# Focal modulation inside a four-block token network: gated maps of two levels added and turned once, rows summed by VectorE, the input turned by 96 products, linear units in 32x32 tiles

## The chip, the cores and the metric

The kernel runs on one core of one Trainium2 chip. The metric is device time in microseconds of one execution. A profile shows five engines: TensorE (PE, its weight loads apart as PEld), VectorE (DVE), ScalarE (ACT), GpSimd (POOL) and SyncE (SP, which here only starts DMAs).

## The reference, cut to what matters

The input is (16, 24, 24, 32): 16 images, 24 x 24 positions, 32 channels. Four blocks follow each other, each with a residual and a norm ahead of it: focal modulation, a recurrence over tokens, a bidirectional state space scan, a mixture of experts. Only the first is changed.

```python
y = einsum('bhwc,cd->bhwd', x, Wf) + bf          # x is the normed input
q, ctx, gates = y[..., :C], y[..., C:2*C], y[..., 2*C:]
ctx_all = 0
for l, k in enumerate((k0, k1, k2)):             # 3x3, 5x5, 7x7, depthwise
    ctx = gelu(dwconv_same(ctx, k))
    ctx_all = ctx_all + ctx * gates[..., l:l+1]
ctx_global = gelu(mean(ctx, axis=(1, 2), keepdims=True))
ctx_all = ctx_all + ctx_global * gates[..., 3:]
x_out = q * (einsum('bhwc,cd->bhwd', ctx_all, Wh) + bh)
x_out = layer_norm(x_out) * gamma + beta         # over channels
x = x + einsum('bhwc,cd->bhwd', x_out, Wp) + bp
```

## The kernel before, in words

Everything stays in on-chip memory. The usual layout, "plain", has partition = group g of images (4) times channel (32), and free = image j in the group (4) times position (576). A position range is worked in two halves a of 288. All products are float32, and each product or weight load of the program leaves two records in the trace.

The first block runs in this order. `ln_pe`, `ln_act` and `ln_dve` are the norm: centring by a product (L391 with full 128x128 tiles, L374 with 32x32 tiles, which also exchanges g and j), a square on ScalarE (L425), a copy (L432), variance (L398), root (L427), reciprocal (L436), spreading (L412) and the final multiplication (L440). `ctx_rows` (L1049) then turns the normed input: for each row y, image j and channel parity c0, a product takes 32 positions as the stationary side and the 76 columns of `wcg` as the moving one, and so writes context channels and gates with the x position on the partitions. `bring_ctx` (L731) adds the bias and moves the result from the banks to `CT0`.

`conv_block` (L1087) does the depthwise convolutions of the three levels with Toeplitz weights in 64x64 tiles, in halves kh of the channels. A record of it has up to 192 moving columns; level 0 has 192 records, level 1 320 and level 2 448. Between blocks, `linear` (L1071) computes q and the part of the global gate in four units of four full products, and `linear_out` (L563) moves each. After each half, ScalarE applies Gelu in two instructions (L571), VectorE multiplies by the gate (`gate`, L750), and after each level VectorE turns the map back with 32x32 transposes in two halves (`turn`, L758). `spread_gates` (L1064) and a ScalarE copy (L556) bring the gates of level 0 and level 2 to the partitions that need them.

After the last convolution TensorE sums the level 2 map over its rows with 48 products against a matrix of ones (L1116). ScalarE takes the Gelu of the mean (L574), VectorE turns and masks it (L766, L770), TensorE makes it a number per channel and image (L1137), and ScalarE moves that (L576). `by_j` (L1122) multiplies the turned maps of the three levels with Wh and adds them up in the banks, one half at a time. VectorE combines this with the global part (L780) and with q (L783) into `XO`, which goes into the next norm. `keep_warm` issues products of zeros (L381) while TensorE would wait.

The order on each engine is the order of the program. SyncE's queue loads, in this order, half of the input, the first weights, the other half, the Toeplitz weights of the three levels, and the weights of later blocks. GpSimd's queue loads `front_in` and `rows_in`. GpSimd computes nothing in the first block but one small fill.

## Time and profile before

| | us |
|---|---|
| median of 3 runs (lowest, highest) | 815.52 (812.94, 819.01) |
| the profiled execution, its time | 813.94 |
| its span, first to last instruction | 812.1 |
| PE busy in the span | 663.8 |
| DVE busy | 619.6 |
| ACT busy | 361.2 |
| POOL busy | 467.7 |
| mean granted TensorE clock | 0.930 of full |

Busy times are sums over the whole kernel, whose blocks have different limits. The first block takes about the first 130 us of the span. A row of a timeline has the start, the time from the first to the last of the merged instructions, the engine, the line, the operation with its operands and shape, the count, and in brackets how long the engine had been idle and what ended that.

### The profile page before, as it was taken

How to read it: one execution, taken by the hardware profiler on the slowest of the kernel's cores; microseconds unless marked ns; L12 is line 12 of the kernel's file. 1: busy time of each engine (PE TensorE's matmuls, PEld its weight loads, DVE VectorE, ACT ScalarE, POOL GpSimd, SP SyncE). 2: the span in 40 equal slices, each digit the busy share in tenths (PEclk: the TensorE clock that was granted, in tenths of full speed). 3: DMA queues.
4: the chain of work that ended last, by engine and by line, in shares of the span. 5: the costliest groups of instructions: out<-in, count | busy, mean ns of one | idle time of the engine just before them, and what ended most of it. 6: DMA issues, size and time to landing. Idle time of an engine off the chain costs nothing. (4 is left out here: it accounts for less than half of the span.)

```text
span 812.1 us, 14545 instructions
## 1 busy us (share of the span) xinstructions
PE 663.8 (82%) x5852; PEld 423.8 (52%) x5852; DVE 619.6 (76%) x664; ACT 361.2 (44%) x569; POOL 467.7 (58%) x239
## 2 busy tenths in 40 slices
PE   7699977899583778988888887898888887786696
PEld 4588933566351455554555555555455454452242
DVE  3254256632431999999999999999999999977765
ACT  2032121566337655645655565565565555422000
POOL 0000000000102899999999999999999999970000
PEclk9799688999798799999999999999999999998577
DMA  9300000000025588797887788778779878710001
GB/s 365 148 3 2 1 2 2 2 0 1 3 74 133 154 209 199 200 227 202 201 227 198 203 226 202 201 205 220 208 200 226 200 204 219 201 47 2 1 17 44
DMA packets 35491, 109.22 MB, mean 134 GB/s; under 512 B 6816, under 2 KB 8992, under 8 KB 35040
## 3 DMA queue, kind: packets, MB, share of 16 engines
q1 hardware_dynamic: 35200, 107.40, 50.4%
q8 instruction: 46, 0.75, 0.4%
q0 software_dynamic: 224, 0.90, 0.3%
q14 instruction: 21, 0.17, 0.1%
HBM read 104.73 MB, written 3.54 MB: 133 GB/s over the span
## 5 line engine op out<-in xcount | busy, mean ns | idle before, releaser
L538 POOL TENSOR_TENSOR ring<-ring,big 128x1152 f32<-128x1152 f32 x74 | 193.9, 2634 | 3.6 <-DVE ring L908 3.6
L197 PE MATMUL banks<-ring,main_params 128*128 128x288 f32 x592 | 173.0, 421 | 0.6 <-POOL ring L538 0.6
L685 ACT ACTIVATE big<-big,small 128x576 f32<-128x576 f32 x192 | 142.5, 765 | 30.4 <-DVE ring L908 15.8
L908 DVE TENSOR_TENSOR_SCAN ring<-big,banks 128x576 f32<-128x576 f32 x111 | 146.1, 1339 | 1.9 <-ACT banks L685 0.4
L896 DVE TENSOR_TENSOR banks<-banks,big 128x576 f32<-128x576 f32 x192 | 141.3, 743 | 1.8 <-POOL big L524 1.6
L1262 PE MATMUL banks<-big,selectors 96*128 96x512 bf16 x192 | 72.5, 389 | 70.5 <-DVE ring L908 40.2
L514 POOL COPY big<-normed 128x288 f32<-128x288 f32 x8 | 3.0, 428 | 214.6 <-DVE normed L440 214.6
L197 PEld LDWEIGHTS banks<-ring,main_params 128*128 128x128 f32 x592 | 104.8, 190 | 35.8 <-issue 3.7
L538 POOL TENSOR_TENSOR normed<-normed,big 128x1152 f32<-128x1152 f32 x36 | 94.6, 2637 | 0.2 <-DVE normed L903 0.2
L197 PE MATMUL banks<-normed,main_params 128*128 128x288 f32 x288 | 83.5, 420 | 0.0
L685 ACT ACTIVATE banks<-big,small 128x576 f32<-128x576 f32 x64 | 47.5, 742 | 79.3 <-DVE ring L908 46.3
L1262 PEld LDWEIGHTS banks<-big,selectors 96*128 96x128 bf16 x192 | 18.5, 96 | 118.5 <-DVE ring L908 59.4
L908 DVE TENSOR_TENSOR_SCAN normed<-big,banks 128x576 f32<-128x576 f32 x54 | 71.2, 1339 | 0.8
L197 PEld LDWEIGHTS banks<-normed,main_params 128*128 128x128 f32 x288 | 51.0, 190 | 16.7 <-issue 1.9
L197 PE MATMUL banks<-big,main_params 128*128 128x288 f32 x208 | 59.6, 416 | 0.0
L381 PE MATMUL banks<-idle 128*128 128x128 bf16 (+1 forms) x172 | 48.0, 341 | 5.6 <-DVE big L968 2.6
L1176 PE MATMUL banks<-big,main_params 128*128 128x90 f32 (+4 forms) x208 | 52.5, 371 | 0.0
L531 POOL TENSOR_TENSOR ring<-big 128x576 f32<-128x576 f32 x37 | 52.1, 1409 | 0.1
L903 DVE TENSOR_TENSOR_SCAN ring<-banks,ring 128x576 f32<-128x576 f32 x37 | 49.6, 1341 | 0.0
L538 POOL TENSOR_TENSOR big<-big 128x1152 f32<-128x1152 f32 x18 | 47.4, 2631 | 0.2 <-DVE big L903 0.2
L518 POOL TENSOR_TENSOR big<-big 128x576 f32<-128x576 f32 x16 | 22.6, 1412 | 38.2 <-ACT big L667 38.2
L197 PEld LDWEIGHTS banks<-big,main_params 128*128 128x128 f32 x208 | 37.3, 190 | 12.0 <-issue 0.9
(186 smaller groups left out, 1043.0 us busy)
## 6 DMA issues: line engine op xcount, KB each, us to landing
big<-bc_rows SPq DMA_DIRECT2D x256, 288.0 KB, 4.4
big<-bc_rows SPq DMA_DIRECT2D x128, 144.0 KB, 4.5
big<-toeplitz_in SPq DMA_DIRECT2D x1, 3584.0 KB, 21.5
bc_rows<-big SPq DMA_DIRECT2D x16, 144.0 KB, 3.5
big<-toeplitz_in SPq DMA_DIRECT2D x1, 1536.0 KB, 10.4
big<-toeplitz_in SPq DMA_DIRECT2D x1, 1280.0 KB, 12.5
residual<-x_in SPq DMA_DIRECT2D x2, 576.0 KB, 5.9
out<-big SPq DMA_DIRECT2D x16, 72.0 KB, 1.8
```

The lines of the kernel that those rows point to most:

```text
L197: last = nc.tensor.matmul(PS[rows, 2 * p + a, 0:HALF], lhsT, rhs[:, bass.ds(at + a * HALF, HALF)], start=start, stop=stop, skip_group_chec ...
L381: nc.tensor.matmul(PS[:, bank, 0:cols], IDLE[:, 0:128], IDLE[:, 0:cols], start=True, stop=True)
L514: nc.gpsimd.tensor_copy(there, XN[:, j * L + a * HALF:j * L + (a + 1) * HALF][:, ::-1]).then_inc(turned, 1)
L518: nc.gpsimd.tensor_tensor(DT[b % 3], DT[b % 3], TMP[b % 2], ALU.add).then_inc(dt_set, 1)
L531: nc.gpsimd.tensor_tensor(SLOT[n % SLOTS], BT[m % 3], DTX[n // DS % 2], ALU.mult).then_inc(u_pool, 1)
L538: nc.gpsimd.tensor_tensor(slots, slots, CT[k % 5], ALU.mult).then_inc(weighted, 1)
L685: nc.scalar.activation(out, DT[b % 3], ACT.Exp, scale=ANEG[:, s:s + 1]).then_inc(decay_set, 1)
L896: nc.vector.tensor_tensor(u, u, DTX[n // DS % 2], ALU.mult).then_inc(u_dve, 1)
L903: nc.vector.tensor_tensor_scan(slot, place, slot, 0.0, ALU.mult, ALU.add).then_inc(scanned, 1)
L908: nc.vector.tensor_tensor_scan(slot, DECAY[m % 3], place, 0.0, ALU.mult, ALU.add).then_inc(scanned, 1)
L1176: nc.tensor.matmul(step_place(k, h), par("vt"), at_step(YP, k, 0, images_of(h)), start=False, stop=True, skip_group_check=True).then_inc(r ...
L1262: nc.tensor.matmul(PS[:, 2 * place, :], lhsT, SPLIT[b % 4][:, 0:BANK], start=True, stop=True)
```

## The change

1. The normed input is written by VectorE into `PADDED`, rows of 32 positions of which 24 are used, two images side by side. GpSimd fills it with zeros first. `ctx_rows` then needs 96 products with 64 stationary columns in place of 192 with 32, and the channel bits stand on other partitions; Toeplitz weights of level 1 double in size, since each half of the partitions has its own.
2. `spread_gates` and its copy go: the gates come out of the turning where they are needed.
3. `linear` uses `strips`, 16 products in 32x32 tiles, which exchange g and j, from `PADDED`; the four units move to other places between the conv blocks. The norm after the modulation so uses full products for the centring, in place of strips.
4. The gated map of level 0 isn't turned: it is added to that of level 2 by VectorE (`add_first`), and the sum is turned. `by_j` has two maps, not three.
5. VectorE sums rows (`sum_rows`, tensor_reduce), and TensorE keeps one product with `sumx`.

```diff
-TW_AT = [0, KS[0] * CP * 64, KS[0] * CP * 64 + KS[1] * KB * 64]
+TW_AT = [0, KS[0] * CP * 64, (KS[0] + KS[1]) * CP * 64]
...
         P0, P1, P2 = CT0[:, 0:TB], A1, B2
-        P0T, P1T = big(TB), big(TB)
+        P1T = big(TB)
+        PADDED = C3
         P2T = P0
         QS = big(N)
         XO = QS
         WPG = big(128)
-        GA = big(2 * 2 * COLS)
-        GG, GGT, GMASK, GADD = big(128), big(128), big(GROUPS * J), big(J)
+        YS, GG, GGT, GMASK, GADD = big(128 + GROUPS), big(128), big(128), big(GROUPS * J), big(J)
...
-        LINEAR = {(1, 0): ("q", 0), (1, 1): ("global", 0), (2, 0): ("q", 1), (2, 1): ("global", 1)}
+        LINEAR = {(0, 1): ("q", 0), (1, 0): ("q", 1), (1, 1): ("global", 0), (2, 0): ("global", 1)}
         LINEARS = list(LINEAR.values())
 
         def by_pair(t):
 
             return t.rearrange("p (n m y) -> p n m y", n=CP, y=H)
+
+        def padded(rows, j, a):
+
+            return PADDED.rearrange("p (b y j x) -> p b j y x", b=2, y=H, j=2)[rows, j // 2, j % 2, a * H // 2:(a + 1) * H // 2, 0:W]
 
...
+                if to_padded:
+                    for b in range(2):
+                        js = slice(2 * b, 2 * b + 2)
+                        here = PADDED.rearrange("p (b y j x) -> p b j y x", b=2, y=H, j=2)[:, b, :, a * H // 2:(a + 1) * H // 2, 0:W]
+                        last = nc.vector.tensor_tensor(here, halves(dst, a)[:, js].rearrange("p j (y x) -> p j y x", x=W),
+                                                       quad(a)[:, js].rearrange("p j (y x) -> p j y x", x=W), ALU.mult)
+                    last.then_inc(ln_out, 1)
+                    continue
...
-            nc.gpsimd.memset(XNW[:, N:N + 8], 0.0).then_inc(tail_zero, 1)
+            nc.gpsimd.memset(PADDED, 0.0).then_inc(pads_zero, 1)
...
-            act.wait_ge(rep_mm, 1)
-            nc.scalar.activation(GA.rearrange("p (l j c) -> p j l c", l=2, j=2),
-                                 PS[:, 4:6, 0:2 * COLS].rearrange("p j (l c) -> p j l c", l=2), ACT.Copy).then_inc(ga_set, 1)
...
-            for kh in range(2):
-                act.wait_ge(sum_mm, kh + 1)
-                nc.scalar.activation(GG[:, 64 * kh:64 * (kh + 1)], PS[:, 4 * kh, 0:64], ACT.Gelu, scale=1.0 / L).then_inc(glob_set, 1)
+            act.wait_ge(sum_mm, 1)
+            nc.scalar.activation(GG, PS[:, 7, 320:448], ACT.Gelu, scale=1.0 / L).then_inc(glob_set, 1)
             act.wait_ge(gadd_mm, 1)
-            nc.scalar.activation(GADD, PS[:, 5, 0:J], ACT.Copy).then_inc(gadd_set, 1)
+            nc.scalar.activation(GADD, PS[:, 7, 448:448 + GROUPS], ACT.Copy).then_inc(gadd_set, 1)
...
-            ln_dve(dve, 0, XN)
+            dve.wait_ge(pads_zero, 1)
+            ln_dve(dve, 0, XN, to_padded=True)
...
-                cols = COLS if l == 1 else 2 * COLS
-                g = CT0[:, (CP + 1) * COLS:(CP + 2) * COLS] if l == 1 else GA[:, l // 2 * cols:(l // 2 + 1) * cols]
+                g = CT0[:, (CP + l) * COLS:(CP + l + 1) * COLS]
+                if l == 1:
+                    dve.wait_ge(gated, 2)
+                dve.wait_ge(ctx_dve, 3)
                 dve.wait_ge(gelu_set, 2 * (2 * l + kh + 1))
-                if l != 1:
-                    dve.wait_ge(ga_set, 1)
-                n = TB // 2 // cols
-                nc.vector.tensor_tensor(dst[:, half].rearrange("p (n c) -> p n c", c=cols),
-                                        src[:, half].rearrange("p (n c) -> p n c", c=cols),
-                                        g.unsqueeze(1).to_broadcast([128, n, cols]), ALU.mult).then_inc(gated, 1)
+                nc.vector.tensor_tensor(dst[:, half].rearrange("p (n c) -> p n c", c=COLS),
+                                        src[:, half].rearrange("p (n c) -> p n c", c=COLS),
+                                        g.unsqueeze(1).to_broadcast([128, CP // 2, COLS]), ALU.mult).then_inc(gated, 1)
...
                 if l == 2:
-                    dve.wait_ge(turned_p, 2)
-                nc.vector.transpose(turned_row((P0T, P1T, P2T)[l], a), by_row((P0, P1, P2)[l], a)).then_inc(turned_p, 1)
+                    dve.wait_ge(added, 2)
+                nc.vector.transpose(turned_row({1: P1T, 2: P2T}[l], a), by_row((P0, P1, P2)[l], a)).then_inc(turned_p, 1)
+
+            nc.vector.memset(YS[:, 128:128 + GROUPS], 0.0).then_inc(summed_c, 1)
+
+            def sum_rows(kh):
+                dve.wait_ge(gelu_set, 2 * (2 * 2 + kh + 1))
+                nc.vector.tensor_reduce(YS[:, 64 * kh:64 * (kh + 1)],
+                                        C3[:, kh * TB // 2:(kh + 1) * TB // 2].rearrange("p (i y) -> p i y", y=H),
+                                        AX.X, ALU.add).then_inc(summed_c, 1)
+
+            def add_first(kh):
+                half = slice(kh * TB // 2, (kh + 1) * TB // 2)
+                dve.wait_ge(gated, 4 + kh + 1)
+                nc.vector.tensor_tensor(P2[:, half], P2[:, half], P0[:, half], ALU.add).then_inc(added, 1)
 
             for l in range(LEVELS):
                 for kh in range(2):
+                    if l == 2:
+                        sum_rows(kh)
                     gate(l, kh)
+                    if l == 2:
+                        add_first(kh)
+                if l == 0:
+                    continue
                 turn(l, 0)
...
-                    dve.wait_ge(glob_set, 2)
+                    dve.wait_ge(glob_set, 1)
...
                 turn(l, 1)
...
-
-            def ctx_rows(ys):
-                for y in ys:
-                    for j in range(J):
+
+            def ctx_rows(a):
+                for y in range(a * H // 2, (a + 1) * H // 2):
+                    for j1 in range(2):
                         for c0 in range(2):
-                            strip = 2 * (j // 2) + c0
-                            here = PS[C * strip:C * (strip + 1), y // 3, 0:3 * CG * 2 * GROUPS]
-                            here = here.rearrange("p (y c q) -> p y c q", y=3, c=CG)[:, y % 3, :, GROUPS * (j % 2):GROUPS * (j % 2 + 1)]
-                            last = nc.tensor.matmul(here, XNW[:, j * L + y * W:j * L + y * W + 32],
-                                                    fpar("wcg")[:, c0 * CG * GROUPS:(c0 + 1) * CG * GROUPS], start=True, stop=True)
+                            w = fpar("wcg")[:, c0 * CG * GROUPS:(c0 + 1) * CG * GROUPS]
+                            here = PS[64 * c0:64 * (c0 + 1), y // 3, 0:3 * CG * 2 * GROUPS]
+                            here = here.rearrange("p (y c q) -> p y c q", y=3, c=CG)[:, y % 3, :, GROUPS * j1:GROUPS * (j1 + 1)]
+                            at = 64 * (j1 * H + y)
+                            last = nc.tensor.matmul(here, PADDED[:, at:at + 64], w, start=True, stop=True)
                 return last
 
-            pe.wait_ge(ln_out, 1)
-            ctx_rows(range(H // 2 - 1))
-            pe.wait_ge(ln_out, 2)
-            ctx_rows([H // 2 - 1]).then_inc(ctx_mm, 1)
-            ctx_rows(range(H // 2, H)).then_inc(ctx_mm, 1)
-
-            def spread_gates():
-                gates = CT0[:, TB:TB + LEVELS * COLS].rearrange("p (l c) -> p l c", l=LEVELS)[:, 0:LEVELS:2, :]
-                pe.wait_ge(ctx_dve, 3)
-                for r in range(2):
-                    rows = slice(64 * r, 64 * r + 32)
-                    last = nc.tensor.matmul(PS[:, 4 + r, 0:2 * COLS], fpar("rep")[rows, :], gates[rows], start=True, stop=True)
-                last.then_inc(rep_mm, 1)
+            for a in range(2):
+                pe.wait_ge(ln_out, a + 1)
+                ctx_rows(a).then_inc(ctx_mm, 1)
 
             def linear(u, q):
                 kind, a = u
                 w = {"q": fpar("wq"), "global": fpar("wg3")}[kind]
-                for j in range(J):
-                    last = nc.tensor.matmul(PS[:, 4 * q + j, 0:HALF], w, XN[:, j * L + a * HALF:j * L + (a + 1) * HALF],
-                                            start=True, stop=True)
+                last = strips(quad_bank(q), own(w), lambda rows, j: padded(rows, j, a), True, True)
                 last.then_inc(lin_mm, 1)
...
-                            n = (dy + KS[l] // 2) * KB + k if l == 1 else (dy + KS[l] // 2) * CP + 2 * k + q
-                            at = TW_AT[l] + 64 * n
+                            at = TW_AT[l] + 64 * ((dy + KS[l] // 2) * CP + 2 * k + q)
...
-                    if (l, kh) == (0, 1):
-                        pe.wait_ge(ga_set, 1)
-                    if l >= 1 and (l, kh) != (1, 0):
-                        pe.wait_ge(lin_act, 2 * l + kh - 2)
+                    if l >= 1:
+                        pe.wait_ge(lin_act, 2 * (l - 1) + kh + 1)
                     for k in range(4 * kh, 4 * kh + 4):
                         last = conv_block(l, kh, k)
-                        if (l, kh, k) == (0, 0, 0):
-                            spread_gates()
                         if (l, kh) in LINEAR and k % 4 == 2:
                             pe.wait_ge(gelu_set, 2 * (2 * l + kh))
                             linear(LINEAR[l, kh], 1 - kh)
                     last.then_inc(tap_mm, 1)
 
+            def by_j(a, g, src, w, start, stop):
+                for j in range(J):
+                    last = nc.tensor.matmul(PS[C * j:C * (j + 1), 4 * a + g, 0:HALF], fpar(w)[:, C * j:C * (j + 1)],
+                                            turned_row(src, a)[:, g, :, 0:W], start=start, stop=stop, skip_group_check=True)
+                return last
+
+            def modulate(a, g):
+                by_j(a, g, P1T, "whb", True, False)
+
+            def finish(a):
+                pe.wait_ge(turned_p, 2 + a + 1)
+                for g in range(GROUPS):
+                    last = by_j(a, g, P2T, "wha", False, True)
+                last.then_inc(mod_mm, 1)
+
             pe.wait_ge(lin_act, len(LINEARS))
-            for kh in range(2):
-                pe.wait_ge(gelu_set, 2 * (2 * 2 + kh + 1))
-                per_row = C3[:, kh * TB // 2:(kh + 1) * TB // 2].rearrange("p (i y) -> p i y", y=H)
-                for y in range(H):
-                    last = nc.tensor.matmul(PS[:, 4 * kh, 0:64], fpar("sumx"), per_row[:, :, y], start=y == 0, stop=y == H - 1)
-                last.then_inc(sum_mm, 1)
-
-            def by_j(a, src, w, start, stop):
-                for j in range(J):
-                    for g in range(GROUPS):
-                        last = nc.tensor.matmul(PS[C * g:C * (g + 1), 4 * a + j, 0:HALF], fpar(w)[:, C * j:C * (j + 1)],
-                                                turned_row(src, a)[:, g, :, 0:W], start=start, stop=stop)
-                return last
-
-            def modulate(a):
-                pe.wait_ge(turned_p, 2 * 1 + a + 1)
-                by_j(a, P0T, "wha", True, False)
-                by_j(a, P1T, "whb", False, False)
-
-            pe.wait_ge(glob_set, 1)
-            modulate(0)
-            pe.wait_ge(turned_p, 2 * 2 + 1)
-            by_j(0, P2T, "wha", False, True).then_inc(mod_mm, 1)
+            pe.wait_ge(gelu_set, 2 * (2 * 2 + 1))
+            pe.wait_ge(turned_p, 2)
+            for g in range(GROUPS):
+                modulate(0, g)
+            pe.wait_ge(summed_c, 3)
+            nc.tensor.matmul(PS[:, 7, 320:448 + GROUPS], fpar("sumx"), YS, start=True, stop=True).then_inc(sum_mm, 1)
+            for g in range(GROUPS):
+                if g == GROUPS - 1:
+                    pe.wait_ge(glob_set, 1)
+                modulate(1, g)
+            finish(0)
             pe.wait_ge(glob_mask, 1)
-            for g in range(GROUPS):
-                last = nc.tensor.matmul(PS[C * g:C * (g + 1), 5, 0:J], fpar("whu"), GMASK[:, g * J:(g + 1) * J],
-                                        start=True, stop=True)
+            for j in range(J):
+                last = nc.tensor.matmul(PS[C * j:C * (j + 1), 7, 448:448 + GROUPS], fpar("whu"),
+                                        GMASK[:, j * GROUPS:(j + 1) * GROUPS], start=False, stop=True, skip_group_check=True)
             last.then_inc(gadd_mm, 1)
             pe.wait_ge(gadd_set, 1)
-            modulate(1)
-            pe.wait_ge(turned_p, 2 * 2 + 2)
-            by_j(1, P2T, "wha", False, True).then_inc(mod_mm, 1)
+            finish(1)
...
-            ln_pe(pe, 1, XO, lambda a: pe.wait_ge(xo_set, a + 1), turn=True, aside=proj_bias)
...
-    whb = np.zeros((2, 2, CP, 2, J, C), f)
+    by_bits = wh.reshape(KB, 2, 2, C)
+    wha, whb, whu = (np.zeros((2, 2, KB, 2, 2, J, C), f) for _ in range(3))
+    jmask = np.zeros((2, 2, KB, 2, 2, J), f)
     for j in range(J):
-        whb[j // 2, :, :, j % 2, j, :] = wh.reshape(CP, 2, C).transpose(1, 0, 2)
+        j1, j0 = j // 2, j % 2
+        wha[:, j0, :, :, j1, j, :] = by_bits.transpose(1, 0, 2, 3)
+        whb[:, j0, :, :, j1, j, :] = by_bits.transpose(2, 0, 1, 3)
+        jmask[:, j0, :, :, j1, j] = 1.0
+    put("wha", wha.reshape(128, 128))
```

## Rows read from the trace of the kernel before

**Rows 1.** Timeline, 18 to 37 us, TensorE and VectorE.

```profile
18.10 2.30 PE L1049 MATMUL banks<-big,normed 128*32 128x76 f32 x123 [1.14 <-DVE normed L440]
...
23.90 4.28 PE L1049 MATMUL banks<-big,normed 128*32 128x76 f32 x128 [3.50 <-issue]
...
30.11 4.09 PE L1049 MATMUL banks<-big,normed 128*32 128x76 f32 x133 [1.92 <-issue]
...
34.24 2.12 DVE L731 TENSOR_TENSOR big<-banks,big 128x768 f32<-128x768 f32 x2 [5.61 <-PE banks L1049]
...
35.34 1.18 PE L1087 MATMUL banks<-big 64*64 64x192 f32 x24 [1.14 <-DVE big L731]
...
36.45 0.91 PE L1064 MATMUL banks<-big 32*128 32x384 f32 x4
```

**Rows 2.** Stretch: time, PE, PEld busy (records), clock, DMA share, GB/s; L1087 alone.

```profile
35.30:82.65 47.35, 38.26 (x960) 35.80 (x960) 1.00 0.01 3
```

**Rows 3.** Timeline: a linear unit, its ScalarE copy, and the conv after it.

```profile
48.77 2.21 PE L1071 MATMUL banks<-normed,big 128*128 128x288 f32 x8
...
50.91 6.42 PE L1087 MATMUL banks<-big 64*64 64x192 f32 x160
51.01 1.23 ACT L563 ACTIVATE big<-banks,big 128x1152 f32<-128x1152 f32 x1 [5.24 <-PE banks L1071]
```

**Rows 4.** Timeline, 82 to 121 us: what follows the last conv record.

```profile
82.63 18.97 PE L1116 MATMUL banks<-big 128*128 128x64 f32 x96
82.77 1.51 ACT L571 ACTIVATE big<-banks 128x768 f32<-128x768 f32 x2 [1.09 <-PE banks L1087]
84.32 1.76 DVE L750 TENSOR_TENSOR big<-big 128x1536 f32<-128x1536 f32 x1 [9.01 <-ACT big L571]
86.11 2.97 DVE L758 STREAM_TRANSPOSE big<-big 128x1536 f32<-128x1536 f32 x1
...
101.53 7.71 PE L1122 MATMUL banks<-big 128*32 128x288 f32 x96
...
109.62 1.79 DVE L780 SCALAR_TENSOR_TENSOR ring<-ring,big,banks 128x288 f32<-128x288 f32 x4 [4.33 <-ACT big L576]
...
109.64 6.18 PE L1122 MATMUL banks<-big 128*32 128x288 f32 x96 [0.35 <-ACT big L576]
...
111.45 1.42 DVE L783 SCALAR_TENSOR_TENSOR big<-ring,big 128x1152 f32<-128x1152 f32 x1
...
119.19 1.27 PE L374 MATMUL banks<-big,main_params 32*32 32x288 f32 x32 [2.65 <-DVE big L783]
120.64 1.13 ACT L425 ACTIVATE ring<-banks 128x1152 f32<-128x1152 f32 x1 [2.80 <-PE banks L374]
```

**Rows 5.** Stretches as rows 2, L1049 alone: before, between and after its holes.

```profile
18.07:20.40 2.33, 2.30 (x123) 2.15 (x124) 1.00 0.95 406
24.00:28.00 4.00, 4.00 (x128) 3.95 (x128) 0.50 0.92 375
30.00:33.00 3.00, 2.90 (x93) 2.89 (x96) 0.50 0.03 5
33.10:34.10 1.00, 0.96 (x48) 0.72 (x37) 1.00 0.00 0
```

**Rows 6.** Stretches as rows 2, L1116 alone.

```profile
82.70:87.60 4.90, 4.90 (x31) 4.90 (x32) 1.00 0.02 3
88.00:101.40 13.40, 13.40 (x64) 13.40 (x63) 0.50 0.00 0
```

**Rows 7.** Groups by line and form: count, busy us, mean ns, idle before.

```profile
L514 POOL COPY big<-normed 128x288 f32<-128x288 f32 x8 | 3.0, 428 | 214.6 <-DVE normed L440 214.6
...
L967 DVE TENSOR_REDUCE big<-big 128x72 f32<-128x576 f32 x1 | 0.8, 753 | 0.0
```

**Rows 8.** The page's DMA issues: size of one, us from issue to landing.

```profile
big<-toeplitz_in SPq DMA_DIRECT2D x1, 3584.0 KB, 21.5
```

**Rows 9.** Timeline: the first centring of norm 1.

```profile
115.76 0.78 PE L374 MATMUL banks<-big,main_params 32*32 32x288 f32 x32
```

More of the change, by code:

```diff
@@ L427, in ln_act, with ln_dve @@
             nc.scalar.activation(STD, PS[:, 0, 0:BLOCK], ACT.Sqrt, bias=EPS[:, eps:eps + 1]).then_inc(ln_std, 1)
-        def ln_dve(dve, n, dst, aside=None):
+        def ln_dve(dve, n, dst, aside=None, to_padded=False):
             for a in range(2):
@@ L777, in _ @@
                 dve.wait_ge(mod_mm, a + 1)
-                for j in range(J):
-                    here = slice(j * L + a * HALF, j * L + (a + 1) * HALF)
-                    nc.vector.scalar_tensor_tensor(out=GLOBAL[:, here], in0=GLOBAL[:, here], scalar=GADD[:, j:j + 1],
-                                                   in1=PS[:, 4 * a + j, 0:HALF], op0=ALU.mult, op1=ALU.add).then_inc(glob_added, 1)
-                dve.wait_ge(glob_added, J * (a + 1))
+                for g in range(GROUPS):
+                    here = slice(g * L + a * HALF, g * L + (a + 1) * HALF)
+                    nc.vector.scalar_tensor_tensor(out=GLOBAL[:, here], in0=GLOBAL[:, here], scalar=GADD[:, g:g + 1],
+                                                   in1=PS[:, 4 * a + g, 0:HALF], op0=ALU.mult, op1=ALU.add).then_inc(glob_added, 1)
+                dve.wait_ge(glob_added, GROUPS * (a + 1))
                 nc.vector.scalar_tensor_tensor(out=halves(XO, a), in0=halves(GLOBAL, a), scalar=fpar("bh"), in1=halves(QS, a),
@@ L1135, in _ @@
+            pe.wait_ge(summed_c, 3)
+            nc.tensor.matmul(PS[:, 7, 320:448 + GROUPS], fpar("sumx"), YS, start=True, stop=True).then_inc(sum_mm, 1)
+            for g in range(GROUPS):
+                if g == GROUPS - 1:
+                    pe.wait_ge(glob_set, 1)
+                modulate(1, g)
+            finish(0)
             pe.wait_ge(glob_mask, 1)
-            for g in range(GROUPS):
-                last = nc.tensor.matmul(PS[C * g:C * (g + 1), 5, 0:J], fpar("whu"), GMASK[:, g * J:(g + 1) * J],
-                                        start=True, stop=True)
+            for j in range(J):
+                last = nc.tensor.matmul(PS[C * j:C * (j + 1), 7, 448:448 + GROUPS], fpar("whu"),
+                                        GMASK[:, j * GROUPS:(j + 1) * GROUPS], start=False, stop=True, skip_group_check=True)
@@ L1419, in lay_out @@
             wcg[g, :, c0, :, g] = wf[:, chans]
-        bcg[:, c0] = bf[chans].reshape(CG, 1, 1)
+        bcg[c0] = bf[chans].reshape(CG, 1, 1)
     put("wcg", wcg.reshape(128, -1))
@@ L1426, in lay_out @@
     wh = a["L0_conv_Wh"]
-    whb = np.zeros((2, 2, CP, 2, J, C), f)
+    by_bits = wh.reshape(KB, 2, 2, C)
+    wha, whb, whu = (np.zeros((2, 2, KB, 2, 2, J, C), f) for _ in range(3))
+    jmask = np.zeros((2, 2, KB, 2, 2, J), f)
     for j in range(J):
-        whb[j // 2, :, :, j % 2, j, :] = wh.reshape(CP, 2, C).transpose(1, 0, 2)
-    put("whb", whb.reshape(128, 128))
-    wha = np.zeros((GROUPS, KB, J, J, C), f)
-    for j in range(J):
-        wha[:, :, j, j, :] = wh.reshape(KB, GROUPS, C).transpose(1, 0, 2)
-    put("wha", wha.reshape(128, 128))
-    put("whu", wha.sum(3).reshape(128, C))
-    put("jmask", np.tile(np.eye(J, dtype=f), (32, 1)))
-    put("rep", np.tile(np.eye(C, dtype=f), (GROUPS, GROUPS)))
+        j1, j0 = j // 2, j % 2
[3 more added lines that the diff above has]
+    put("wha", wha.reshape(128, 128))
+    put("whb", whb.reshape(128, 128))
+    put("whu", wha.sum(5).reshape(128, C))
+    put("jmask", jmask.reshape(128, J))
     put("sumx", blocks(np.ones((C, C), f)))
@@ L1447, in lay_out @@
                     t[xi, :, :, xo] = taps[:, xi - xo + KS[l] // 2, :]
-        pairs = np.zeros((2, 32, KS[l], CP, 2, 32), f)
+        bits = t.reshape(32, KS[l], KB, 2, 2, 32)
+        bits = bits.transpose(3, 0, 1, 2, 4, 5) if l == 1 else bits.transpose(4, 0, 1, 2, 3, 5)
+        pairs = np.zeros((2, 2, 32, KS[l], CP, 2, 32), f)
         for r in range(2):
-            pairs[r, :, :, :, r, :] = t[:, :, r::2, :]
-        pairs = pairs.reshape(64, KS[l], CP, 64)
-        by_half = (pairs[:, :, 0::2], pairs[:, :, 1::2]) if l == 1 else (pairs, pairs)
-        t = np.concatenate([h.reshape(64, -1) for h in by_half], 0)
+            pairs[:, r, :, :, :, r, :] = bits.reshape(2, 32, KS[l], CP, 32)
+        t = pairs.reshape(128, -1)
         toeplitz.append(t)
```

21 lines of the change are left out of this document (10 added, 11 removed).

## The prediction

> **What bounds the kernel now.** The change touches only the first of the kernel's five parts, the focal modulation, so the page's chain of waits, whose longest pieces lie behind 670 us, says nothing about it. I read the timeline of the first 125 us instead, and ask of each stretch which engine the next step waits for. There are three stretches.
>
> Second, the convolutions, 35.3 to 82.7: TensorE is never idle [rows 2, 3], while VectorE and ScalarE wait for it. Of 47.4 us, 38.3 are the 960 records of L1087 (39.9 ns each) [rows 2], 0.9 is the spreading of the gates (L1064) [rows 1], and the rest the four linear units (L1071, 2.13 us from the start of one to the next conv block).
>
> Third, the tail, from the last conv record at T = 82.7. TensorE sums rows with L1116 until 101.5, then mixes the turned maps (L1122, in all 192 records); VectorE can start XO only at 109.62, and the second centring of the next norm reaches ScalarE at 120.64, T + 37.9 [rows 4]. From there on the code is the same in both kernels. I sum up to this event.
>
> **The change part by part.**
>
> *Turning the input.* 192 products with 32 weight columns become 96 with 64. This isn't half of the work: the stationary side doubles, and two tiles, not four, share the array. A record took 18.9 ns at the full clock and 31 ns at half [rows 5]. For 128x64 tiles with 76 moving columns no row exists. L1087 gives 39.9 x 4 / 192 = 0.83 ns per moving column and tile, so 76 columns stream in 63 ns and two tiles give at best 32 ns a record. L1116 (128 weight columns, 64 moving) took 153 ns at the full clock [rows 6]; 53 of it is streaming, so 100 is loading, 50 for 64 columns: loading and streaming one after another give (50 + 63) / 2 = 57 ns. The old form, by the same working (25 + 63) / 4 = 22, took 18.9, 0.86 of it, so I take 48 ns, nearest to that row. 192 records then need 9.2 us at the full clock, against 7.3 before: on its own this edit costs 2 us. What it saves is the holes. Half as many instructions pass, and slower, so record 124 is reached at 18.1 + 124 x 0.048 = 24.1 us, when the stream of before was there again (23.9); the next 128 records end in the convolution at about 31, against an arrival at 30.1 before. With 9.2 us, or 12 if the clock drops for the second half, the turning ends between 27.3 and 30; one bias move (1.1 us) follows and the convolution starts at 28.4 to 31; I take 29.3, **6.0 us earlier**. The bounds are 27.3 (32 ns, first hole kept) and 35.
>
> The Trainium skill (TensorE: Matmul & The Clock Gate, "LDWEIGHTS (loading the stationary operand)") says that a load's time goes with its columns, P / 1.2 ns. It speaks against this edit: 64 columns would be 53 ns a record, 10.2 us for 192, 1 us above my sum; L1116's 100 ns for 128 agrees with it, L1049's 18.9 ns for 32 columns doesn't as long as loads may not overlap (27 by the rule).
>
> The normalised input is now written into padded rows by two instructions per half instead of one of 1.35 us, at most 0.15 more. The fill of PADDED on GpSimd (3072 columns) is bounded above by its copy, 428 ns for 288 columns, so 4.6 us [rows 7]: over by 7.2, before VectorE's first norm copy at 10.8. The middle Toeplitz part doubles, 1.3 MB more at the 400 GB/s of this stretch: 3.3 us later than before for what lies behind it in the queue; the last part (21.5 us from issue [rows 8]) comes at 28 and is wanted at 58. Costed at nothing.
>
> *Gate spreading.* L1064 with its scalar copy goes; conv blocks take its place: **0.9 us**. The gates for every channel half come out of the turning.
>
> *Linear units.* Four of 2.13 us [rows 3] become 32 records in 32x32 tiles; L374 does the same shape in 0.78 at the full clock, 1.27 at half [rows 9]. I take 0.85: 4 x 1.28 = **5.1 us**. One now stands in the short level 0: only one block of 24 records (1.0 us) follows before level 1 wants its banks, while ScalarE's copy takes 1.22, so a stall of 0.4. The conv stretch is then 38.3 + 3.4 + 0.4 = 42.1 us and T = 71.4.
>
> *The tail.* L1116's 19.0 us on TensorE go. In their place VectorE sums rows twice; L967 reduces 576 columns in 753 ns [rows 7], so 1536 take at most 2.0 us; L750's 1.76 for 1536 is the lower side; I take 1.75. VectorE adds level 0 to level 2 (as L750, 1.76) twice and loses the two turns of level 0 (2.87 each, hidden under the convolutions). The halves for kh = 0 fit into the 8.6 us of the last conv half. Then after T: Gelu 1.6, sum 1.75, gate 1.8, addition 1.8, turn 3.0: T + 10.0; transpose, mask, second turn: T + 13.4. **VectorE is now the bound.** TensorE has the level 1 mixing (64 records, 4 us) and one sum product under this, then idles some 4 us until T + 10. After 3.5 idle us in the first stretch it was at 1.2 GHz when work came back [rows 1, 5], so I expect the half clock here. 32 records of L1122 took 2.1 us at full [rows 4]; at half 3.5 to 4. So first half mixed T + 13.5, global sum through ScalarE T + 14.2, four L780 and L783 [rows 4] T + 17.4 for XO's first half; second half mixed by T + 17.5, XO ready at T + 20.7. Centring is now 8 full products, 16 records for two halves (8 records 2.1 us at full [rows 3], 4.2 at half) in place of L374: it ends at T + 22.9 to 26.2. I take **T + 24.0**, against T + 37.9.
>
> Sum: the event moves from 120.6 to 71.4 + 24.0 = 95.4, 25.2 us earlier. The profiled execution took 813.94 us with a span of 812.1; that is 1.6 below the median of 815.52. 813.94 - 25.2 = 788.7, 815.52 - 25.2 = 790.3; I say 789. Nothing behind the event waits for a load that started before it, so I expect nothing to be given back, but a shift of the clock's steps can move the rest by 2 us.
>
> The Trainium skill (the same page, "HAM oscillation") says that idle gaps bring the array's clock down, so a change that empties TensorE pays with slower work after. Without any drop the tail would be T + 22.5, with all of it at half T + 26.5. The trace adds that busy isn't enough: during L1116 the clock fell to half with TensorE busy throughout [rows 6].
>
> **The rivals.**
> - *Weight loads serialise with the streaming*: 57 ns at full and 88 at half, (50 + 127) / 2: 96 records 5.5 us, 96 at half 8.5, conv start at 33.2 instead of 29.3: 793. For it: L1116's sum is exact. Against: L1049 ran 14% below it. The Trainium skill's rule quoted above points the same way.
> - *The tail stays at half clock and VectorE's queue slips* (turns late, centring at T + 27, a further 2 us in the conv start from a clock that comes back late): 794 to 797.
> - *All goes well*: 32 ns records, no stall, no clock drop: conv start 27.3, T = 69.3, event T + 22.5 = 91.8: 785. A point below it lies within 2 us for the rest.
> - *Slower*: the sparse turning leaves the clock at 1.2 GHz when the convolutions start, and 64x64 tiles don't lift it. Each L1087 record would take 80 ns in place of 40. It decides from 25.2 / 0.04 = 630 of the 960 records; all of them give 827. Against: at 33 us the clock rose during sparser work than this [rows 5].
> - *The edit doesn't shorten the tail*: another chain behind 82.7 as long as the sums. None is in the rows; VectorE idles from 89 to 101.9 us. Would be 803.
>
> **How the numbers follow.** Forecast (786 to 792) 0.56; serial loads 0.13; slow tail 0.13; all well 0.13; slower 0.02; unshortened 0.03. The range 781 to 798 leaves about 1 to 2 in 10 out with the kernel's own scatter (812.9 to 819.0). Faster by over 1% holds all but the slower case and a remnant: 0.96; within 1% (what a measurement of this kernel can tell from nothing) 0.02; slower 0.02.
>
> **What would show it.** Turning records near 48 ns, no hole of 3 us in them, conv start near 29; no L1064 or L1116; linear units 0.8 to 1.2; the last conv record near 71; VectorE without a gap from there to the second turn; the half clock at the mixing; ScalarE's second square of norm 1 near 95. Wrong would be: holes that stay, conv records at 80 ns, or VectorE's reductions well over 2 us.

## The result and the profile after

| | before | after |
|---|---|---|
| median, us | 817.26 (4 runs, 812.94 to 821.57) | 790.25 (4 runs, 783.06 to 792.87) |
| profiled execution | 813.94 | 783.06 |
| its span | 812.1 | 781.2 |

The ratio is 0.966, 95% interval 0.957 to 0.974: 27 us less. The profiled execution of after is its fastest, so its span gains more (30.9 us) than the median. Of all executions reported here one, the 792.6 us of experiment 9, was in a slower state of the chip; the ratios leave it out.

The turning in the timeline of after (L1075 is the turning, L739 the bias move, L1099 the convolution), to be laid beside [rows 1]:

```profile
17.85 4.27 PE L1075 MATMUL banks<-big 128*64 128x76 f32 x123 [1.20 <-DVE big L448]
...
23.88 2.46 PE L1075 MATMUL banks<-big 128*64 128x76 f32 x69 [1.76 <-issue]
...
26.39 2.12 DVE L739 TENSOR_TENSOR big<-banks,big 128x768 f32<-128x768 f32 x2 [3.00 <-PE banks L1075]
...
27.50 7.16 PE L1099 MATMUL banks<-big 64*64 64x192 f32 x168 [1.15 <-DVE big L739]
```

"Issue" in the brackets is idle time that waits for nothing the profile shows. There is one such hole of 1.76 us instead of two of 3.5 and 1.9. It ends at 23.88, as the first one did before (23.90): what follows record 123 is there at the same moment, and TensorE only needs it later. A record takes 34.7 ns (4.27 / 123). The windows view (stretch, its length, busy of each engine with its records, then the granted clock as a share of 2.4 GHz, the DMA share and GB/s) shows that the clock never fell in this execution, where [rows 5] had 0.50, which is 1.2 GHz:

```profile
17.85:22.20 4.35, 4.27 (x123) 4.15 (x124) 2.04 (x3) 0.00 (x0) 0.00 (x0) 1.00 1.00 426
22.20:23.88 1.68, 0.00 (x0) 0.00 (x0) 1.20 (x1) 0.00 (x0) 0.00 (x0) 1.00 1.21 512
23.88:26.40 2.52, 2.46 (x69) 2.31 (x68) 0.01 (x1) 0.00 (x0) 0.00 (x0) 1.00 0.87 375
```

A linear unit, its copy on ScalarE and the convolution around it (timeline of after; [rows 3] before):

```profile
34.59 0.77 PE L378 MATMUL banks<-big 32*32 32x288 f32 x32
...
35.29 1.19 PE L1099 MATMUL banks<-big 64*64 64x192 f32 x24
35.55 1.22 ACT L571 ACTIVATE big<-banks,big 128x1152 f32<-128x1152 f32 x1 [2.18 <-PE banks L378]
...
36.91 4.87 PE L1099 MATMUL banks<-big 64*64 64x192 f32 x120 [0.43 <-ACT big L571]
```

From the unit's start to the next conv block it is 0.70 us, where it was 2.14. The unit in level 0 makes the next level wait 0.43 us for ScalarE's copy.

The tail in the timeline of after, from the last conv record at T = 69.2 ([rows 4] before):

```profile
69.16 2.20 PE L1121 MATMUL banks<-big 128*32 128x288 f32 x32
69.27 1.51 ACT L579 ACTIVATE big<-banks 128x768 f32<-128x768 f32 x2 [6.96 <-PE banks L1099]
70.82 1.75 DVE L771 TENSOR_REDUCE big<-big 128x64 f32<-128x1536 f32 x1 [3.26 <-ACT big L579]
72.49 1.75 DVE L757 TENSOR_TENSOR big<-big 128x1536 f32<-128x1536 f32 x1
...
74.27 1.76 DVE L778 TENSOR_TENSOR big<-big 128x1536 f32<-128x1536 f32 x1
76.14 2.77 DVE L765 STREAM_TRANSPOSE big<-big 128x1536 f32<-128x1536 f32 x1
...
78.96 3.67 PE L1121 MATMUL banks<-big 128*32 128x288 f32 x32 [3.71 <-DVE big L765]
...
79.33 2.89 DVE L765 STREAM_TRANSPOSE big<-big 128x1536 f32<-128x1536 f32 x1
...
82.98 1.79 DVE L806 SCALAR_TENSOR_TENSOR ring<-ring,big,banks 128x288 f32<-128x288 f32 x4 [0.76 <-ACT big L583]
83.00 2.20 PE L1121 MATMUL banks<-big 128*32 128x288 f32 x32 [0.31 <-ACT big L583]
...
91.69 1.13 ACT L429 ACTIVATE ring<-banks 128x1152 f32<-128x1152 f32 x1 [1.96 <-PE banks L395]
```

From the reduction to the end of the second turn VectorE has no gap worth naming, and TensorE waits 3.71 us for it: the two engines have changed places. Behind that wait the 32 records of the mixing take 3.67 us where the same 32 took 2.20 at 69.16, and the granted clock is near half:

```profile
79.00:82.70 3.70, 3.70 (x40) 1.75 (x40) 3.19 (x3) 0.00 (x0) 0.00 (x0) 0.56 0.00 0
```

The event to which I summed, the second square of norm 1, comes at 91.69 instead of 120.64.

| stretch, us | before | after | difference | forecast |
|---|---|---|---|---|
| start to first conv record | 35.34 | 27.50 | -7.84 | -6.0 |
| convolutions | 47.37 | 41.72 | -5.65 | -5.3 |
| tail to the second square | 37.93 | 22.47 | -15.46 | -13.9 |
| the rest of the span | 691.5 | 689.5 | -2.0 | 0, give or take 2 |

### The profile page after: what moved, and what is told of

It reads as the page before. It is cut to its first block and busy times, and to the rows that moved or that the text cites. A ratio compares the mean times of both kernels' runs of the same rounds, so it can differ in the third digit from the quotient of the medians.

```text
span 781.2 us, 13931 instructions
## 1 busy us (share of the span) xinstructions
PE 627.6 (80%) x5540; PEld 397.6 (51%) x5546; DVE 620.8 (79%) x669; ACT 360.3 (46%) x567; POOL 469.9 (60%) x239
## 5 line engine op out<-in xcount | busy, mean ns | idle before, releaser
L1271 PEld LDWEIGHTS banks<-big,selectors 96*128 96x128 bf16 x192 | 18.5, 96 | 118.2 <-DVE ring L934 59.1
L385 PE MATMUL banks<-idle 128*128 128x128 bf16 (+1 forms) x166 | 43.9, 320 | 7.4 <-DVE big L994 2.6
L530 POOL TENSOR_TENSOR big<-big 128x576 f32<-128x576 f32 x16 | 22.5, 1408 | 40.0 <-ACT big L674 40.0
```

The costliest lines, as they stand in the source:

```text
L385: nc.tensor.matmul(PS[:, bank, 0:cols], IDLE[:, 0:128], IDLE[:, 0:cols], start=True, stop=True)
L530: nc.gpsimd.tensor_tensor(DT[b % 3], DT[b % 3], TMP[b % 2], ALU.add).then_inc(dt_set, 1)
L1271: nc.tensor.matmul(PS[:, 2 * place, :], lhsT, SPLIT[b % 4][:, 0:BANK], start=True, stop=True)
```

## Experiments

All start from the changed kernel, but the fourth from the kernel before. Medians belong to several runs each, but the seventh is a single execution; positions come from one profiled execution. The granted clock of a stretch is from the windows view. A difference of 1 or 2 us is read off the position of the second square, since the medians scatter by more.

**1. Narrow turning again.** 192 products with 32 stationary columns, from the padded rows:

```diff
-here = PS[64 * c0:64 * (c0 + 1), y // 3, 0:3 * CG * 2 * GROUPS]
...
-at = 64 * (j1 * H + y)
-last = nc.tensor.matmul(here, PADDED[:, at:at + 64], w, start=True, stop=True)
+for j0 in range(2):
+    strip = 2 * c0 + j0
+    here = PS[C * strip:C * (strip + 1), y // 3, 0:3 * CG * 2 * GROUPS]
...
+    at = 64 * (j1 * H + y) + 32 * j0
+    last = nc.tensor.matmul(here, PADDED[:, at:at + 32], w, start=True, stop=True)
```

> The changed kernel, but the input is turned by 192 products with 32 stationary columns again, from the padded rows. My theory (the edit gains by fewer instructions in the stretch, not by TensorE work): records near 19 ns at the full clock, a hole of 3 to 4 us after some 124 records and a second one of about 2 us, the half clock after the first, and the convolution starts at 34 to 36 us instead of 27.5; the median is 6 to 8 us above the changed kernel. Rival (wide tiles save TensorE time, the holes are chance): the convolution starts within 2 us of 27.5.

Measured: median 793.9 us (790.8 to 799.0), ratio 0.970 (0.965 to 0.976). The timeline of this kernel:

```profile
17.91 2.27 PE L1077 MATMUL banks<-big 128*32 128x76 f32 x123 [1.20 <-DVE big L448]
23.97 3.48 PE L1077 MATMUL banks<-big 128*32 128x76 f32 x128 [3.79 <-issue]
...
29.90 2.31 PE L1077 MATMUL banks<-big 128*32 128x76 f32 x128 [2.45 <-issue]
33.36 0.33 PE L1077 MATMUL banks<-big 128*32 128x76 f32 x5 [1.15 <-issue]
...
34.84 8.56 PE L1101 MATMUL banks<-big 64*64 64x192 f32 x168 [1.15 <-DVE big L739]
```

The records are nearly twice as fast at the full clock (18.5 ns against 34.7), and the convolution starts 7.3 us later all the same. So the wide tiles save hardly any TensorE work: 384 x 18.5 = 7.1 us against 192 x 34.7 = 6.7. They save holes, each after another 123 to 128 records, and the half clock behind the first hole (128 records in 3.48 us, then in 2.31). The clock is at half once more when the convolutions start and until about 38.5, so they take 43.1 us against 41.7, and the second square comes 9.2 us later, at 100.84. The median rose by only 3.7 us, less than half of that and below the 6 to 8 I expected; both kernels scatter by 8 to 10 us.

**2, 3 and 4. Late loads.** What SyncE loads behind the level 0 Toeplitz weights waits until the turning is done; in the changed kernel, in the narrow form of experiment 1, and in the kernel before:

```diff
 part = slice(TW_AT[l], (TW_AT + [TW_W])[l + 1])
+if l == 1:
+    sp.wait_ge(ctx_mm, 2)
```

> The changed kernel, but everything behind the level 0 Toeplitz weights in SyncE's queue is loaded only after the turning. If the hole of 1.8 us in the turning is the instruction stream held up by the initial loads, it goes and the convolution starts at 25.7 to 26 us; if it is a fixed latency of that stream, the hole stays at 1.5 us or more. The level 1 weights, 2.6 MB, then land at 33, before level 1 wants them at 36.9, so nothing else should move.

> 32 stationary columns, 192 products, and the late loads. If the loads hold up the instruction stream: the first hole shrinks from 3.5 to about 2 us (what the second hole of the kernel before had without loads), a second and third of about 2 stay, since 128 records need only 2.4 us; the convolution starts at 30 to 32. If loads don't matter: as the run with 192 products without late loads.

> The kernel before, with the late loads alone. By the instruction stream theory the first hole shrinks from 3.5 to about 2 us, the clock drop may be spared, and the convolution starts 1.5 to 5 us earlier than 35.3. By the rival nothing moves there.

Medians 790.0 (ratio 0.964, 0.956 to 0.971), 794.1 (0.971, 0.964 to 0.978) and 814.2 (0.997, 0.993 to 1.001). First the changed kernel with late loads, timeline:

```profile
18.13 6.54 PE L1077 MATMUL banks<-big 128*64 128x76 f32 x192 [1.20 <-DVE big L448]
25.81 6.88 PE L1101 MATMUL banks<-big 64*64 64x192 f32 x168 [1.14 <-DVE big L741]
32.63 1.40 PE L378 MATMUL banks<-big 32*32 32x288 f32 x32
...
40.38 1.45 PE L1101 MATMUL banks<-big 64*64 64x184 f32 x30 [1.00 <-issue]
...
46.65 3.92 PE L1101 MATMUL banks<-big 64*64 64x176 f32 x94 [1.14 <-issue]
```

The hole in the turning is gone, and the convolution starts at 25.8, in the range that I had given for this cause. But two holes of "issue" now stand inside the convolutions, where the after kernel has none: at 39.4 while the late loads run, and at 45.5 as they run out. Counted from the start of the turning they stand behind records 506 and 634, again 128 apart, and a shorter stop of 0.6 us, 128 records earlier, makes the linear unit at 32.63 take 1.40 us instead of 0.77. The conv stretch grows from 41.7 to 45.1 at the full clock, so all of the gain is given back and more (second square at 93.21, 1.5 us later). The holes follow the loads; on which path the loads hold the instructions up no run shows. I hadn't foreseen that; "nothing else should move" was wrong.

The kernel before with late loads:

```profile
18.14 2.30 PE L1051 MATMUL banks<-big,normed 128*32 128x76 f32 x123 [1.14 <-DVE normed L440]
21.46 2.32 PE L1051 MATMUL banks<-big,normed 128*32 128x76 f32 x128 [1.02 <-issue]
24.92 2.32 PE L1051 MATMUL banks<-big,normed 128*32 128x76 f32 x128 [1.15 <-issue]
28.39 0.36 PE L1051 MATMUL banks<-big,normed 128*32 128x76 f32 x5 [1.15 <-issue]
29.88 2.15 PE L1089 MATMUL banks<-big 64*64 64x192 f32 x24 [1.14 <-DVE big L733]
```

Its holes are 1.0 to 1.2 us each, not the 2 that I expected: what I took for the free latency of that stream ([rows 1], 1.9 us) must still have had some of the load in it. The pieces of 128 records start 3.46 us apart (21.46, 24.92, 28.39), while under the loads it was 6.2 in the kernel before (23.90 to 30.11) and 5.9 in experiment 1. A hole is what is left of this interval when 128 records take less: 2.3 us for narrow records, 4.4 for wide ones, 5.1 for conv records. That is why the wide form has no hole without loads, and why the convolutions have some under loads.

The convolution starts 5.5 us earlier (29.88), the clock stays full in the turning, and yet the last conv record comes only 1.5 us earlier, at 81.2. Here it isn't the holes that give the gain back (one of 0.26 us is marked) but the clock. The windows of the conv records alone:

```profile
29.80:32.00 2.20, 2.12 (x24) 1.45 (x24) 0.50 0.93 312
34.00:36.00 2.00, 2.00 (x32) 1.62 (x28) 0.50 1.08 453
38.00:40.00 2.00, 2.00 (x60) 1.82 (x56) 1.00 1.06 459
```

It is at half from the start of the convolutions to about 36.5, which is 6.7 us of records at half speed; the stretch takes 51.3 us instead of 47.4.

The narrow form with late loads has holes of 1.2, 1.4 and 1.2 us in the turning; its first norm ended 1.8 us later in that execution (start of the turning 19.70), so from there to the convolution it took 12.1 us against 16.9 in experiment 1. Its convolutions took 47.6 against 43.1, with a hole of 1.67 us under the late loads and the half clock behind it:

```profile
51.05 8.10 PE L1103 MATMUL banks<-big 64*64 64x192 f32 x158 [1.67 <-issue]
```

**5. Sums on TensorE again.**

```diff
-sum_rows(kh)
...
-nc.tensor.matmul(PS[:, 7, 320:448 + GROUPS], fpar("sumx"), YS, start=True, stop=True)
...
+for kh in range(2):
...
+    per_row = C3[:, kh * TB // 2:(kh + 1) * TB // 2].rearrange("p (i y) -> p i y", y=H)
+    for y in range(H):
+        nc.tensor.matmul(PS[:, 4 * kh, 0:64], fpar("sumx"), per_row[:, :, y], start=y == 0, stop=y == H - 1)
```

> The changed kernel, but TensorE sums the rows again (96 records of 128x128 with 64 columns), VectorE doesn't. Second square of norm 1 in the changed kernel: T + 22.5. The sums take 15 to 19 us on TensorE, and the mask, the global number and the second half's mixing come after them: T + 33 to T + 38. If VectorE were the bound in the tail all the same, as in the rival that another chain is as long, T + 22 to T + 25. Median 11 to 15 us above the changed kernel, or no change.

Measured: median 802.2 (796.9 to 805.5), ratio 0.982 (0.977 to 0.986), 12 us above the changed kernel. Last conv record at 68.7, second square at 105.58, T + 36.8. Its timeline:

```profile
68.67 19.42 PE L1136 MATMUL banks<-big 128*128 128x64 f32 x96
...
88.02 8.50 PE L1118 MATMUL banks<-big 128*32 128x288 f32 x96
...
105.58 1.13 ACT L429 ACTIVATE ring<-banks 128x1152 f32<-128x1152 f32 x1 [1.96 <-PE banks L395]
```

Bringing the sums back lengthens the tail by 14.4 us, of the 15.5 that it had lost.

By chance the same profile tests the hole in the turning. Its first norm ended 1.7 us late, and the turning ran through under full loads without a hole, since record 123 ended only at about 23.9, when the next piece was there anyway; the convolution started at 27.27, no later than the 27.50 of the changed kernel:

```profile
19.59 6.54 PE L1072 MATMUL banks<-big 128*64 128x76 f32 x192 [1.20 <-DVE big L448]
```

**6 and 11. Three maps turned**, level 0 under the convolutions into the dead level 0 weights, mixed by TensorE; the last group of the second half is mixed behind the global number:

```diff
-P1T = big(TB)
+P0T, P1T = TW[:, 0:TB], big(TB)
...
-                    if l == 2:
-                        add_first(kh)
-                if l == 0:
-                    continue
...
+                by_j(a, g, P0T, "wha", True, False)
-                by_j(a, g, P1T, "whb", True, False)
+                by_j(a, g, P1T, "whb", False, False)
```

> The changed kernel, but the level 0 map is turned by itself under the convolutions and mixed by TensorE, as before, in place of being added by VectorE. If VectorE is the bound of the tail, as I hold, this part of the change costs time: one addition of 1.8 us leaves the path, the 64 records more on TensorE fit into its idle 4 us: second square at T + 20 to T + 21 instead of T + 22.5, the first half mixed at the full clock. If TensorE's work is what counts: T + 24 to T + 27. The median moves by 2 us at most, near its scatter.

> Level 0 turned by itself, once more: event at 89.1, 2.6 us before the changed kernel. A median 1 to 4 us below that of the changed kernel if the later stages are alike; if the earlier 782.4 holds beside a changed kernel at 790, something behind the event differs too.

Measured: medians 782.4 (780.8 to 787.2; ratio 0.961, 0.957 to 0.964) and 784.2 (782.3 to 785.9; 0.960, 0.958 to 0.962). Second square at 89.14 and 89.35, T + 19.9 in the first. Its timeline:

```profile
69.16 4.20 PE L1117 MATMUL banks<-big 128*32 128x288 f32 x64
...
73.71 3.22 PE L1117 MATMUL banks<-big 128*32 128x288 f32 x48
74.28 2.98 DVE L765 STREAM_TRANSPOSE big<-big 128x1536 f32<-128x1536 f32 x1
...
77.31 2.20 PE L1117 MATMUL banks<-big 128*32 128x288 f32 x32 [0.37 <-DVE big L765]
```

The turn starts 1.9 us earlier, TensorE's wait shrinks from 3.71 to 0.37 us, and its mixing runs at the full clock. This part of the change costs time: without it the event comes 2.3 to 2.6 us earlier than in the first profile of the changed kernel, and 1.5 to 1.7 us earlier than in its second one (experiment 9), which had the full clock too. The medians are 5 to 8 us lower than those of the changed kernel, more than the 2 I allowed and more than the event explains; experiment 9 comes back to this.

**7. Full products in the linear units.** q and the global gate come out unexchanged here, so they meet another image's modulator.

```diff
-last = strips(quad_bank(q), own(w), lambda rows, j: padded(rows, j, a), True, True)
+for j in range(J):
+    last = nc.tensor.matmul(PS[:, 4 * q + j, 0:HALF], w, padded(slice(0, 128), j, a), start=True, stop=True)
```

> The changed kernel, but each linear unit is four full 128x128 products (q and the global gate then come out with images and groups not exchanged, so they meet another image's modulator). By my sum a unit takes 2.1 us instead of 0.7 to 0.8, and the conv stretch is 4 x 1.35 = 5.4 us longer, 47 instead of 41.7 us; the rival, that the padded rows of 24 read slower in small tiles than in full ones, would give less than 4.

Measured, one execution of 794.0 us: conv stretch 46.97 us (29.53 to 76.50), 5.25 above the changed kernel; a unit takes 2.16 us from its start to the next block. The rival, under 4 us, falls. The clock dropped in this one's turning, which is why its convolution starts 2 us late; that is no effect of the edit, which comes later. It shows that the wide turning doesn't always keep the full clock: behind a hole of 2.10 us its last 69 records took 4.10 us instead of 2.46, the only one of the seven profiles of the wide form with a hole there in which that happened.

```profile
24.27 4.10 PE L1075 MATMUL banks<-big 128*64 128x76 f32 x69 [2.10 <-issue]
```

**8 and 10. Idle products in the tail**, 60 of 128 columns, before the first half is finished:

```diff
+for _ in range(60):
+    nc.tensor.matmul(PS[:, 6, 384:512], IDLE[:, 0:128], IDLE[:, 0:128], start=True, stop=True, skip_group_check=True)
 finish(0)
```

> The changed kernel with 60 idle products of 128 columns while TensorE waits for the first turn of level 2. If the idling is what lowers the clock there, the first half's mixing takes 2.2 us instead of 3.7 and the second square comes at T + 21 to T + 21.5; if the clock falls for another reason, no change.

> The kernel with 60 idle products in the tail once more. The event gains 0.8 us over the changed kernel. If the 8 us between the medians (782.6 against 790.3) are chance in the later clock, the two come out within 3 us of each other here; if the idle products set the later clock, this one stays near 783.

Measured: medians 782.6 (782.1 to 783.3; ratio 0.960, 0.957 to 0.964) and 784.4 (781.1 to 788.5; 0.961, 0.959 to 0.964). Both profiled executions have the mixing at 2.20 us and the second square at T + 21.6 and T + 21.7, 0.1 to 0.2 above my range.

**9. The changed kernel once more.**

> The changed kernel itself once more, beside the next two on one chip: its executions spread over 783 to 793 us while the second square of norm 1 should again come at 91.7. If the spread belongs to stages behind the change (TensorE's clock after the recurrence and in the experts), the event stays within 0.5 us (but for the starting loads) and the rest of the span varies by up to 8 us.

Measured: median 789.4 (780.6 to 792.6; 788.1 without the slowest), ratio 0.965 (0.961 to 0.969). The second square comes at 90.87, 0.8 earlier than in the first profile, more than the 0.5 I allowed, and the timeline says why:

```profile
79.04 2.20 PE L1121 MATMUL banks<-big 128*32 128x288 f32 x32 [3.71 <-DVE big L765]
```

```profile
79.00:81.30 2.30, 2.24 (x40) 1.18 (x40) 2.27 (x3) 0.00 (x0) 0.00 (x0) 1.00 0.00 0
```

The same wait of 3.71 us, and no half clock behind it. So the wait makes the drop possible, not certain: in the six profiles with this wait (after, experiments 1, 2, 3, 7 and 9) the mixing took 3.5 to 4.1 us five times and 2.2 once; in the two with idle products, 2.2 both times. That fits the idea that idling lowers the clock, and the drop is worth 0.9 us here (T + 22.5 against T + 21.6), but two executions don't prove that the idle products prevent it: the event comes no earlier with them than in this execution without them.

The spread lies behind the change. The experts' stage of two executions, each from the last of GpSimd's weighings (after, then experiment 2; windows view):

```profile
697.70:781.20 83.50, 57.28 (x927) 26.59 (x928) 56.96 (x78) 5.12 (x7) 2.62 (x2) 0.84 0.06 16
```

```profile
702.50:790.70 88.20, 64.91 (x927) 28.55 (x928) 57.05 (x78) 5.11 (x7) 2.61 (x2) 0.73 0.06 15
```

The same 927 records, 0.84 against 0.73 of the clock, 4.7 us. The stage between the recurrence and the first scan adds as much: 62.2 us in after, 67.6 in experiment 2 and 65.5 in experiment 9.

Is one kernel luckier there than another? From the second square to the end, the profiled executions took 689.5 and 695.2 us for the changed kernel, 689.3 and 696.1 with the idle products, 691.9 and 694.8 with three maps. The same kernel differs from itself by 3 to 7 us, and no kernel stands out. The medians must also be laid beside the kernel before of their own group of runs, whose median was 817.3 with the first runs of the changed kernel, 814.3 with experiments 6 and 8, and 815.5 with experiments 9 to 11. By the ratios, experiments 6, 8, 10 and 11 lie 0.004 to 0.006 below the changed kernel, 3 to 5 us, of which the event explains 0 to 3. The rest stays open, and the intervals overlap. My two outcomes for experiment 10 were medians within 3 us of each other or this one near 783; they came out 5 us apart (3.7 without the slowest), with this one at 784.4, which decides nothing.

## Why the prediction was right

The time was forecast at 789 and came out at 790; all three stretches moved the forecast way. Part of this closeness is luck. The stretches gained 28.95 us where I summed 25.2. From the 815.5 that I started from, that would be a median of about 787; but it lies 7.2 us above the profiled execution, where that of the kernel before lies 3.3 above its own: the rest of the span, with its clock, scatters by more than what I was off.

*Turning the input*: that the gain is in the holes and not in TensorE's work was right (experiment 1), though the edit by itself saves 0.4 us of that work, where I had it cost 2. The mis-sized term is the record, 34.7 ns where I took 48. It lies next to the bound from streaming alone (32), so hardly any of the loading shows in it; carrying the old form's 0.86 over to the wide tile was the error. With faster records the first hole stayed, 1.76 us, which I had only in the lower bound. Together 8.5 us (17.85 to 26.34) stand where I had 9.2 to 12. *Weight loads serialise* (57 ns) is refuted for this form.

The Trainium skill's load rule (TensorE: Matmul & The Clock Gate, "LDWEIGHTS (loading the stationary operand)") gives 53 ns as the time of one load of 64 columns. The trace has a record every 35, so read as the least time from one record to the next in column tiles, as I read it, it doesn't hold here.

*The hole's cause* was inferred from counts only. Experiments 2 and 4 show that the loads make the holes long, since the holes go or shrink without them and come up where the loads are moved to. That what arrives late is the instruction stream stays a reading: it rests on the label "issue" and on the step of 128 records, which holds across all lines, from the turning into the convolutions.

*Gates and linear units*: 5.65 against 5.3 us; a unit is 0.70 where I took 0.85, the stall 0.43 where I took 0.4. Experiment 7 gives 5.25 for the units alone, against 5.1 by my sum. (The parts that I gave for the stretch before, 38.3, 0.9 and four times 2.13, add up to 47.7 and not to 47.4; so the gains part by part, 0.9 + 5.1 - 0.4 = 5.6, and the 5.3 that I summed with differ by 0.3.)

*The tail*: reductions 1.75 us each, as taken. VectorE as the bound: shown by experiment 6, where one addition less brings the turn forward by its own length. The half clock came (3.67 us), but only over the first half's mixing; the second half's and the centring ran at full. So T + 22.5 belongs beside my lower bound for that course, T + 22.9, and not beside the T + 24.0 that I took, 1.1 us of which were for a half clock in the centring. Without a drop the tail is T + 21.6 (experiment 9), where I had 22.5: the first turn ended at T + 9.7 and not T + 10, the second at T + 13.0 and not T + 13.4.

What I missed: that "added, then turned once" is a loss of 1.5 to 2.6 us in this place. I had priced both sides, 1.8 us for an addition on the path and TensorE idle for 4, and didn't draw the conclusion.

The other rivals: *slower* needed conv records at 80 ns; they ran at 40. Where the convolutions did start at the half clock (experiments 1 and 4), it was full again after 3.7 and 6.7 us. *The edit doesn't shorten the tail* is refuted by 15.5 us. *All goes well*, with its event at 91.8, is what happened up to the event, although none of its conditions (32 ns records, no stall, no clock drop) held in full. Its 785 fits the profiled execution (783.1) and not the median.

## What to carry to other kernels

When a stretch of many small products has holes that wait for nothing, count records from hole to hole: a constant count points to instructions that arrive late. Then compare the time that so many records take with the interval at which they arrive; fewer, fatter instructions close the hole even where the engine's own work stays the same. Moving the sums from TensorE to an idle VectorE paid 14.4 us here although VectorE then became the engine that the others wait for; once it is, look again at each step that was given to it and at the engine that now waits. Delaying bulk loads out of one stretch put their cost into the next one here. And where the same kernel scatters by 8 us, read a gain of 2 us off the position of an event, in more than one profile.

## What the runs showed of the hardware

Small float32 products came in pieces of 123 to 128 records. Without bulk loads the pieces started 3.5 to 3.7 us apart (experiments 3 and 4), under them 5.9 to 6.2 (experiment 1 and the kernel before). The holes of the narrow form were 1.0 to 1.4 us without loads beside them; the first hole was 3.5 to 3.8 us under them, that of the wide form 1.7 to 2.1 or none. The 128x64 form with 76 moving columns takes 34.7 ns a record, the 128x32 form 18.5, both at the full clock. Summing 1536 columns by rows of 24 takes VectorE 1.75 us, as long as a multiplication of as many columns. A TensorE wait of 3.71 us was followed by the half clock in five of six profiles, so one execution more or less tells nothing about such a step.
